# A fused block on one core: in self-attention's last round, the order of weights, values and gate products is changed

## The chip, the cores and the metric

The kernel runs on one core of a Trainium2 chip. The metric is device time in microseconds (us); three runs of the kernel before gave a median of 600.7 us (600.48 to 602.36). The core's engines have a queue of instructions each: TensorE (PE, matrix products; PEld is its loading of weights), VectorE (DVE), ScalarE (ACT), GpSimd (POOL) and SyncE (SP, which starts most transfers). They wait for each other by semaphores.

## The reference, cut to what matters

`x` has 64 time steps of 32 sequences with 256 channels, so 2048 rows; `ctx_768` holds 257 context rows for each time step.

```python
x = x + cross_attention(layernorm(x), ctx_768, ...)      # 16 heads
x = x + self_attention(layernorm(x), W, proj, concat_w, concat_b)
x = x + moe_ffn(layernorm(x), Wg, W1, b1, Wo, bo)         # 8 experts, top 2

def self_attention(inputs, W, proj, concat_w, concat_b):  # inputs (64, 32, 256)
    hp = tanh(einsum('sbh,hk->sbk', inputs, W))
    scores = einsum('sbk,k->sb', hp, proj)
    logits = where(s < t, scores[s, b], most negative float)
    attn = softmax(logits, axis=1)                        # over s
    context = einsum('tsb,sbh->tbh', attn, inputs)
    out = tanh(einsum('tbc,hc->tbh', concatenate([inputs, context], -1), concat_w) + concat_b)
    return out.at[:2].set(inputs[:2])
# moe_ffn starts with gate_logits = einsum('btd,ed->bte', x, Wg), softmax, top_k(2)
```

## The kernel before, in words

The program has three long stages: cross-attention (to 336 us of the profiled span), self-attention together with the gate of the experts (337 to 428 us, with the loads of the expert weights beside it), and the experts with the final sums. The change is in the second one, in a stretch of 13 us of it.

Self-attention takes the 2048 rows in four chunks of 512 (four tiles of 128 rows). All work is written as a pipeline of rounds `k = 0..5`, the same loop on each engine. In round k, chunk `c = k - 1` goes through attention and chunk `k - 2` through its third layernorm and the gate. Each engine works strictly through the order in which its calls are written; nothing reorders them but the code itself. So in round 4 the attention of the last chunk (chunk 3) and the gate of chunk 2 stand side by side, and in round 5 only the gate of chunk 3 and what follows it are left.

The pieces that the change touches, by their names in the code:

- On TensorE: `direct` (the product of the inputs with the first half of concat_w, left open in two PSUM banks), `crossed` (turns the attention weights Ab, four transposes), `mixed` (adds weights times values into the open banks: four matmuls; two increments of `u_o`, one for each half), `lifted` (turns the normed rows yn of a chunk for the gate, eight transposes in two halves), `gated` (the gate product, one half of it for each half of lifted), `turned_back` (turns its result gc, one transpose). Behind them in round 5 stand `slots(1)` (eight small matmuls that find the rows' positions), `busy(2)` (two matmuls with no use for the result, they only keep TensorE at work), `raised` (turns the last chunk's rows), `busy(1)`, `weighed` (the gate product of the last chunk), and `rank`.
- On VectorE: `weighted` (reciprocal and the product that makes Ab; waits for the exponentials), `values` (adds the bias to `products`' result and so makes Yv, two instructions), `positions` and `marks` (index arithmetic for the expert slots of a chunk two rounds earlier), `third` (adds self-attention's result to xb, then mean and variance), `best` and `chosen` (the top 2 of the gate).
- On ScalarE: `weights` (copies the turned weights to AT), `outs` (the two tanh of the result, zs), `gate_in` (copies the two halves of lifted to gh), `gate_out` (copies the gate product to gc).

For one chunk the way is: exponentials (ACT), weighted (DVE), crossed (PE), weights (ACT), mixed (PE), outs (ACT), third (DVE), scales (POOL). For the gate of a chunk: lifted, gate_in, gated, gate_out, turned_back, best.

PSUM has eight banks. Seven of them are given out in turn by a list, `plan`: the n-th tile of the list has bank n mod 7 and, before it is written, `take` waits for the semaphore with which the tile seven places before it was read out. The list and the order of the calls on TensorE have to agree.

At the end of the stage VectorE writes the list `inv` of rows by expert; GpSimd's first gather waits for it, and the experts for that gather.

Of the kernel before, what the change touches and what calls it, by code (L numbers as in the profile page):

```python
# [76 lines left out]
def build(nc, d, out, vx_d, w1_d, y_d, g_d):  # L77
    ctx = ExitStack()
    with ctx:
# [242 lines left out]
        u_ate = sem("u_ate")  # L322
# [45 lines left out]
        for k in range(6):  # L368
            c = k - 1
            if 0 <= c < 4:  # L370
                plan += [(("h", c, m), u_he, 2 * c + m + 1) for m in range(2)]
            if k < 4:
                plan += [(("t", k, h), u_tl, 2 * k + h + 1) for h in range(2)]
            if 0 <= c < 4:
                plan += [(("s", c), u_l, c + 1)]
            if k < 2:
                plan += [(("y", a, h), u_x, 2 * a + h + 1) for a, h in ahead[k + 1]]
            if 0 <= c < 4:
                plan += [(("Y", c, h), u_yb, 2 * c + h + 1) for h in range(2)]
            if 0 <= k - 3 < 2:  # L380
                plan += [(("r", k - 3), u_rk, k - 2)]
            if 0 <= c < 4:
                plan += [(("ay", c, h), u_z, 2 * c + h + 1) for h in range(2)]
            if k == 5:
                plan += [(("idle",), u_o, 8)]
            if 0 <= k - 2 < 4:
                plan += [(("t3", k - 2, h), f_hi, 2 * (k - 2) + h + 1) for h in range(2)]
            if 0 <= c < 4:
                plan += [(("at", c), u_ate, c + 1)]
            if 0 <= k - 2 < 4:  # L390
                plan += [(("g", k - 2), f_gl, k - 1)]
            if k == 5:
                plan += [(("r", 2), u_rk, 3), (("inv",), r_iv, 1)]
# [172 lines left out]
        with nc.Block() as block:  # L566
# [647 lines left out]
            def _(t):  # L1214
# [87 lines left out]
                def mixed(c):  # L1302
                    t.wait_ge(u_ate, c + 1)
                    t.wait_ge(u_yb, 2 * c + 2)
                    for h in range(2):
                        b = bank("ay", c, h)
                        for jj in range(2):
                            j = 2 * h + jj
                            mm = t.matmul(b[:, C * jj:C * jj + C], AT[:, j, :], Yv[:, j, :],
                                          start=False, stop=(jj == 1), skip_group_check=True)  # L1310
                        mm.then_inc(u_o, 1)
# [59 lines left out]
                for k in range(6):  # L1371
                    c = k - 1
                    if 0 <= c < 4:
                        hidden(c)
                    if 0 <= k - 4:
                        slots(t, k - 4)
                    if k < 4:
                        turned(k)
                    if 0 <= c < 4:
                        logits(c)  # L1380
                    if k < 2:
                        attended(ahead[k + 1])
                    if 0 <= c < 4:
                        products(c)
                    if 0 <= k - 3 < 2:
                        rank(t, k - 3, take("r", k - 3))
                    if 0 <= c < 4:
                        direct(c)
                    if k == 5:
                        take("idle")  # L1390
                        busy(2)
                        raised()
                        busy(1)
                        weighed()
                    if 0 <= k - 2 < 3:
                        lifted(k - 2)
                    if 0 <= c < 4:
                        crossed(c)
                    if 0 <= k - 2 < 3:
                        gated(k - 2)  # L1400
                    if 0 <= c < 4:
                        mixed(c)
                    if 0 <= k - 2 < 3:
                        turned_back(k - 2)
                b = take("r", 2)
# [14 lines left out]
            def _(v):  # L1420
# [38 lines left out]
                def final_norm(c):  # L1459

                    if c:
                        v.wait_ge(f_t, 2 * c)
                        v.wait_ge(f_yd, 16 * c + 16)
                    v.wait_ge(f_r, 3 * c + 2)
                    for j in range(2):
                        n = 4 * c + j
                        v.tensor_scalar(yn[:, j, :], xb[:, n, :], mv[:, n, 0:1], rs[:, n:n + 1],
                                        ALU.subtract, ALU.mult).then_inc(f_yv, 1)
# [8 lines left out]
                def values(c):  # L1477
                    for h in range(2):
                        v.wait_ge(u_yp, 2 * c + h + 1)
                        if c:  # L1480
                            v.wait_ge(u_o, 2 * c)
                        v.tensor_tensor(Yv[:, 2 * h:2 * h + 2, :], bank("Y", c, h)[:, :].rearrange("p (a c) -> p a c", a=2),
                                        bcc[:, 1, :].unsqueeze(1).broadcast_to([128, 2, C]), ALU.add).then_inc(u_yb, 1)
# [11 lines left out]
                def weighted(c):  # L1495
                    v.wait_ge(u_ex, 4 * c + 4)
                    link(v.reciprocal(sm[:, 2, :], sm[:, 1, :]))
                    v.wait_ge(u_az, 1)
                    if c:
                        v.wait_ge(u_at, c)  # L1500
                    for h in range(2):
                        r = slice(64 * h, 64 * h + 64)
                        v.tensor_tensor(Ab[r, :, 64 * h:64 * h + 64], L[r, :, :],
                                        sm[r, 2, :].unsqueeze(2).broadcast_to([64, 4, 64]), ALU.mult).then_inc(u_a, 1)
# [68 lines left out]
                for k in range(6):  # L1573
                    if 0 <= k - 2 < 4:
                        third(k - 2)
                    if k < 4:
                        lowered(k)
                    if 0 <= k - 1 < 4:
                        masked(k - 1)
                    if k < 4:  # L1580
                        kept(k)
                    if k == 5:
                        best(2)
                        chosen(2)
                        best(3)
                        chosen(3)
                    if 0 <= k - 2 < 2:
                        final_norm(k - 2)
                    if 0 <= k - 1 < 4:
                        weighted(k - 1)  # L1590
                        values(k - 1)
                    if 0 <= k - 3 < 2:
                        positions(v, link, k - 3, bank("r", k - 3))
                    if k == 5:
                        positions_of_two(v, link, bank("r", 2))
                    if k == 0:
                        added(((2, 0), (2, 1), (3, 0)))
                        moments(2)
                    if k == 1:
                        added(((3, 1),))  # L1600
                        moments(3)
                    if 0 <= k - 3:
                        marks(v, k - 3)
                    if 0 <= k - 2 < 2:
                        best(k - 2)
                        chosen(k - 2)
# [37 lines left out]
            def _(a):  # L1644
                a.wait_ge(s_ote, T)

                def normed(c):
                    a.wait_ge(u_rs, c + 1)
                    if c:
                        a.wait_ge(u_t, 2 * c)  # L1650
                        a.wait_ge(u_b2, c)
                    for j in range(2 * (c == 0), 4):
                        n = 4 * c + j
                        a.activation(xn[:, j, :], xb[:, n, :], ACT.Identity, bias=nb[:, 0, n:n + 1],
                                     scale=rs[:, n:n + 1]).then_inc(u_xn, 1)
# [61 lines left out]
                for k in range(6):  # L1717
                    if 0 <= k - 1 < 4:
                        squashed(k - 1)
                    if k < 4:  # L1720
                        highs(k)
                    if 0 <= k - 1 < 4:
                        exps(k - 1)
                    if 0 <= k - 2 < 3:
                        final_norm(k - 2)
                    if k + 1 < 4:
                        normed(k + 1)
                    if 0 <= k - 2 < 4:
                        gate_in(k - 2)
                    if k == 5:  # L1730
                        final_norm(3)
                    if 0 <= k - 1 < 4:
                        weights(k - 1)
                    if 0 <= k - 2 < 3:
                        gate_out(k - 2)
                    if 0 <= k - 1 < 4:
                        outs(k - 1)
                a.wait_ge(u_rf, 3)
                a.wait_ge(u_iv, 2)
# [326 lines left out]
```

## Time and profile before

| | |
|---|---|
| three runs, median (lowest to highest) | 600.7 us (600.48 to 602.36) |
| profiled execution: its time | 600.85 us |
| profiled execution: its span | 599.0 us |
| PE busy, share of the span | 583.1 us, 97% |
| DVE | 461.3 us, 77% |
| ACT | 351.0 us, 59% |
| POOL | 329.7 us, 55% |
| granted TensorE clock, mean | 0.994 |
| granted clock, 410 to 420 us and 420 to 430 us | 0.90 and 0.76 |

The 1.85 us between time and span lie around the recorded instructions. Matmul records overlap, so TensorE's share says that something was nearly always in it, not that it was at its peak; the filler matmuls of `busy` count as work too. An idle time in brackets at the end of a row is that of the engine just ahead of the instruction, with what ended it.

### The profile page before, as it was taken

How to read it: one execution, taken by the hardware profiler on the slowest of the kernel's cores; microseconds unless marked ns; L12 is line 12 of the kernel's file. 1: busy time of each engine (PE TensorE's matmuls, PEld its weight loads, DVE VectorE, ACT ScalarE, POOL GpSimd, SP SyncE). 2: the span in 40 equal slices, each digit the busy share in tenths (PEclk: the TensorE clock that was granted, in tenths of full speed). 3: DMA queues.
4: the chain of work that ended last, by engine and by line, in shares of the span. 5: the costliest groups of instructions: out<-in, count | busy, mean ns of one | idle time of the engine just before them, and what ended most of it. 6: DMA issues, size and time to landing. Idle time of an engine off the chain costs nothing.

```text
span 599.0 us, 21927 instructions
## 1 busy us (share of the span) xinstructions
PE 583.1 (97%) x8431; PEld 480.6 (80%) x8431; DVE 461.3 (77%) x1072; ACT 351.0 (59%) x768; POOL 329.7 (55%) x481
## 2 busy tenths in 40 slices
PE   8999999999999999999999999998899999999996
PEld 3888878888788888788888788886388878777695
DVE  4688867888678887677777687689778888887584
ACT  3677868878588888577777164545333333332462
POOL 3456867788668787678875222111346666664000
PEclk9999999999999999999999999999899999999999
DMA  8724553766544946693610399165424333344892
GB/s 230 182 68 119 149 188 94 242 162 213 153 148 147 264 118 219 167 247 125 210 41 4 125 435 400 65 204 198 156 95 132 133 131 134 130 131 126 314 343 75
DMA packets 65398, 102.13 MB, mean 170 GB/s; under 512 B 15280, under 2 KB 41968, under 8 KB 64400
## 3 DMA queue, kind: packets, MB, share of 16 engines
q1 hardware_dynamic: 59440, 84.59, 44.6%
q0 software_dynamic: 4992, 15.34, 7.7%
q8 instruction: 70, 1.15, 0.8%
q10 hardware_dynamic: 864, 0.79, 0.5%
q14 instruction: 32, 0.26, 0.1%
HBM read 69.43 MB, written 31.27 MB: 168 GB/s over the span
## 4 chain that ended last, share of the span: by engine, by line
PE 49%; POOL 20%; issue 15%; DVE 7%; DMA 4%; ACT 4%; DVEq 1%; POOLq 0%; SPq 0%; ACTq 0%
PE bank L1974 5%; PE bank L1048 5%; PE bank L1055 5%; PE bank L1080 4%; POOL hA L722 4%; POOL lA L718 4%; PE bank L2002 4%; POOL hA L714 4%; PE scores L1096 3%; PE scores L1069 3%; PE scores L1974 2%; DVE sg L1802 2%; DVE gg L1811 2%; PE scores L1232 2%; ACT sg L1916 2%
## 5 line engine op out<-in xcount | busy, mean ns | idle before, releaser
L854 DVE TENSOR_SCALAR Pm<-scores 128x514 f32<-128x514 f32 x128 | 88.1, 688 | 52.8 <-PE scores L1069 52.4
L970 ACT ACTIVATE Pm<-Pm,nm 128x257 f32<-128x257 f32 x256 | 115.8, 505 | 2.5 <-DVE nm L859 2.5
L859 DVE TENSOR_REDUCE nm<-Pm 128x2 f32<-128x514 f32 x128 | 87.5, 684 | 2.2
L965 ACT ACTIVATE PT<-bank 128x512 f32<-128x512 f32 x64 | 38.3, 598 | 74.3 <-PE bank L1080 74.3
L1048 PE MATMUL bank<-hA,wH 128*128 128x258 f32 x256 | 75.1, 304 | 0.3 <-POOL hA L722 0.3
L1080 PE MATMUL bank<-cst,Pm 128*128 128x128 f32 x512 | 70.0, 279 | 0.0
L1048 PE MATMUL bank<-hA,wL 128*128 128x258 f32 x256 | 69.2, 281 | 0.0
L1055 PE MATMUL bank<-wH,hA 128*128 128x256 f32 x256 | 68.9, 281 | 0.0
L1055 PE MATMUL bank<-wL,hA 128*128 128x256 f32 x256 | 68.8, 280 | 0.0
L1974 PE MATMUL bank<-W,xh 128*128 x208 | 66.8, 402 | 0.5 <-ACT xh L1904 0.5
L755 POOL TENSOR_TENSOR Mb<-Os,rc 128x64 f32<-128x64 f32 x64 | 21.8, 340 | 73.8 <-DVE rc L879 73.4
L1096 PEld LDWEIGHTS scores<-Vs,PT 128*32 128x32 f32 x4096 | 41.3, 110 | 26.1 <-issue 25.1
L1916 ACT ACTIVATE sg<-sg 128x512 f32<-128x512 f32 x39 | 24.7, 632 | 62.7 <-DVE sg L1802 62.7
L1789 POOL DMA_INDIRECT g_d<-gg,ds x39 | 38.6, 989 | 37.1 <-DVE gg L1811 37.1
L1080 PEld LDWEIGHTS bank<-cst,Pm 128*128 128x128 f32 x512 | 54.8, 140 | 2.8 <-issue 0.8
L948 ACT ACTIVATE kT<-bank,bcol 128x258 f32<-128x258 f32 x128 | 53.7, 470 | 2.9 <-PE bank L1048 2.6
L1778 POOL DMA_INDIRECT Xg<-y_d,inv x39 | 38.1, 977 | 24.3 <-DVE inv L1619 12.7
L1048 PEld LDWEIGHTS bank<-hA,wH 128*128 128x128 f32 x256 | 48.4, 189 | 1.5 <-issue 1.4
L1048 PEld LDWEIGHTS bank<-hA,wL 128*128 128x128 f32 x256 | 48.5, 190 | 0.2 <-issue 0.2
L1096 PE MATMUL scores<-Vs,PT 128*32 128x17 f32 x4096 | 47.8, 186 | 0.8 <-issue 0.6
L1055 PEld LDWEIGHTS bank<-wH,hA 128*128 128x128 f32 x256 | 48.1, 188 | 0.0
L1055 PEld LDWEIGHTS bank<-wL,hA 128*128 128x128 f32 x256 | 48.1, 188 | 0.0
(289 smaller groups left out, 1453.6 us busy)
## 6 DMA issues: line engine op xcount, KB each, us to landing
w_d<-whl SPq DMA_DIRECT2D x64, 256.0 KB, 3.6
W<-w_d SPq DMA_DIRECT2D x6, 2048.0 KB, 17.5
wst<-in_W1T SPq DMA_DIRECT2D x32, 256.0 KB, 3.8
cg<-g_d SPq DMA_DIRECT2D x16, 512.0 KB, 6.2
cx<-in_ctxT SPq DMA_DIRECT2D x31, 258.0 KB, 3.0
cx<-in_ctxT SPq DMA_DIRECT2D x62, 129.0 KB, 3.5
bb<-in_b SPq DMA_DIRECT2D x8, 512.0 KB, 6.5
W<-w_d SPq DMA_DIRECT2D x5, 512.0 KB, 5.2
```

The costliest lines, as they stand in the source:

```text
L854: v.tensor_scalar(Pm[:, i % 2, 2 * p:2 * p + 2, :], S4[:, 2 * p:2 * p + 2, 0:NK], -CLAMP, CLAMP, ALU.max, ALU.min).then_inc(s_cl, 1)
L859: v.tensor_reduce(nm[:, i % 2, 2 * p:2 * p + 2], Pm[:, i % 2, 2 * p:2 * p + 2, :], AX.X, ALU.max, negate=True).then_inc(s_nm, 1)
L948: a.activation(kT[:, i % 2, m, :], held("k", i, m)[:, 0:NKP], ACT.Identity, bias=bcol[:, 2 + m:3 + m]).then_inc(s_ke, 1)
L965: a.activation(PT[:, i % 2, 0, :, :].rearrange("p a b -> p (a b)"), held("p", i, 0)[:, :], ACT.Copy).then_inc(s_pte[0], 1)
L970: a.activation(Pm[:, i % 2, g, :], Pm[:, i % 2, g, :], ACT.Exp, bias=nm[:, i % 2, g:g + 1]).then_inc(s_ex, 1)
L1048: mm = t.matmul(b[:, 0:NKP], w[:, 128 * m:128 * m + 128], c, start=(e == 0), stop=(e == 4))
L1055: mm = t.matmul(b[:, C * c:C * c + C], x[:, 128 * c:128 * c + 128], w[:, C:2 * C], start=(e == 0), stop=(e == 4))
L1080: mm = t.transpose(b[:, o:o + 128], Pm[:, i % 2, 2 * p + gg, 128 * c:128 * c + 128], ident)
L1096: mm = t.matmul(pO[r, VH * g:VH * g + VH], PT[:, i % 2, p, 2 * gg + c, r], Vs[:, i % 4, c, 4 * (h // 2) + g, h % 2, :], start=first, stop= ...
L1778: g.indirect_dma_start(out=Xg[:, i % 4, :], out_offset=None, in_=y_d, in_offset=bass.IndirectOffsetOnAxis(ap=inv[:, i:i + 1], axis=0)).the ...
L1789: g.indirect_dma_start(out=g_d, out_offset=bass.IndirectOffsetOnAxis(ap=ds[:, i:i + 1], axis=0), in_=gg[i % 3][:, :], in_offset=None).then ...
L1974: mm = t.matmul(o, x[:, i % 3, k, :], W1[:, bass.DynSlice(w + (part * 2048 + k * 1024 + 512 * h), 512)], start=(k == 0 and part == 0 and x ...
```

## The change

Three things are written in another order, and nothing is computed otherwise. On TensorE, in round 4, `crossed(3)` and `mixed(3)` stand ahead of `lifted(2)` and `gated(2)`; before, the order was lifted(2), crossed(3), gated(2), mixed(3). `turned_back(2)` stays behind all of them. The plan of the banks is changed to agree. On VectorE `values(3)` stands ahead of `weighted(3)`. On ScalarE `weights(3)` and `outs(3)` stand ahead of `gate_in(2)`; `gate_out(2)` now follows gate_in(2) directly.

```diff
--- before.py
+++ after.py
@@ -383,9 +383,11 @@
                 plan += [(("ay", c, h), u_z, 2 * c + h + 1) for h in range(2)]
             if k == 5:
                 plan += [(("idle",), u_o, 8)]
+            if k == 4:
+                plan += [(("at", c), u_ate, c + 1)]
             if 0 <= k - 2 < 4:
                 plan += [(("t3", k - 2, h), f_hi, 2 * (k - 2) + h + 1) for h in range(2)]
-            if 0 <= c < 4:
+            if 0 <= c < 3:
                 plan += [(("at", c), u_ate, c + 1)]
             if 0 <= k - 2 < 4:
                 plan += [(("g", k - 2), f_gl, k - 1)]
@@ -1392,14 +1394,17 @@
                         raised()
                         busy(1)
                         weighed()
-                    if 0 <= k - 2 < 3:
+                    if 0 <= k - 2 < 2:
                         lifted(k - 2)
                     if 0 <= c < 4:
                         crossed(c)
-                    if 0 <= k - 2 < 3:
+                    if 0 <= k - 2 < 2:
                         gated(k - 2)
                     if 0 <= c < 4:
                         mixed(c)
+                    if k == 4:
+                        lifted(2)
+                        gated(2)
                     if 0 <= k - 2 < 3:
                         turned_back(k - 2)
                 b = take("r", 2)
@@ -1586,8 +1591,11 @@
                         chosen(3)
                     if 0 <= k - 2 < 2:
                         final_norm(k - 2)
+                    if k == 4:
+                        values(3)
                     if 0 <= k - 1 < 4:
                         weighted(k - 1)
+                    if 0 <= k - 1 < 3:
                         values(k - 1)
                     if 0 <= k - 3 < 2:
                         positions(v, link, k - 3, bank("r", k - 3))
@@ -1725,15 +1733,18 @@
                         final_norm(k - 2)
                     if k + 1 < 4:
                         normed(k + 1)
+                    if k == 4:
+                        weights(3)
+                        outs(3)
                     if 0 <= k - 2 < 4:
                         gate_in(k - 2)
                     if k == 5:
                         final_norm(3)
-                    if 0 <= k - 1 < 4:
+                    if 0 <= k - 1 < 3:
                         weights(k - 1)
                     if 0 <= k - 2 < 3:
                         gate_out(k - 2)
-                    if 0 <= k - 1 < 4:
+                    if 0 <= k - 1 < 3:
                         outs(k - 1)
                 a.wait_ge(u_rf, 3)
                 a.wait_ge(u_iv, 2)
```

TensorE, the end of round 4 and the start of round 5, the kernel before (yn: lifted; Ab: crossed; gh with a 32-row result: gated; Yv,AT: mixed; gc: turned_back; A_114,Bv: slots(1); cst alone: busy; xb: raised):

```order
L1343 MATMUL bank<-cst,yn 128x128 x4
L1343 MATMUL scores<-cst,yn 128x128 x4
L1299 MATMUL scores<-cst,Ab 128x128 x4
L1351 MATMUL scores<-gh,WgT 32x128 x8
L1309 MATMUL bank<-Yv,AT 128x256 x4
L1362 MATMUL scores<-cst,gc 128x128
L436 MATMUL bank<-A_114,Bv 128x128 x8
L1367 MATMUL scores<-cst 128x512 x2
L1320 MATMUL bank<-cst,xb 128x128 x8
```

The same place in the changed kernel:

```order
L1301 MATMUL bank<-cst,Ab 128x128 x4
L1311 MATMUL bank<-Yv,AT 128x256 x4
L1345 MATMUL scores<-cst,yn 128x128 x8
L1353 MATMUL scores<-gh,WgT 32x128 x8
L1364 MATMUL scores<-cst,gc 128x128
L438 MATMUL bank<-A_114,Bv 128x128 x8
L1369 MATMUL scores<-cst 128x512 x2
L1322 MATMUL bank<-cst,xb 128x128 x8
```

The turned weights and their product have moved to the front; the three steps of the gate (yn, gh, gc) now follow each other with nothing between them, and slots, fillers and raised stand behind them as before.

ScalarE at the same place, before (yn: final_norm(2); gh: gate_in; AT: weights; gc: gate_out; zs: outs):

```order
L1664 ACTIVATE yn<-xb,nb,rs 128x256 x4
L1714 ACTIVATE gh<-bank 128x512
L1714 ACTIVATE gh<-scores 128x512
L1693 ACTIVATE AT<-scores 128x512
L1700 ACTIVATE gc<-scores 128x128
L1707 ACTIVATE zs<-bank 128x512 x2
L1714 ACTIVATE gh<-bank 128x512 x2
```

and in the changed kernel:

```order
L1672 ACTIVATE yn<-xb,nb,rs 128x256 x4
L1701 ACTIVATE AT<-bank 128x512
L1715 ACTIVATE zs<-bank 128x512 x2
L1722 ACTIVATE gh<-scores 128x512 x2
L1708 ACTIVATE gc<-scores 128x128
L1722 ACTIVATE gh<-bank 128x512 x2
```

The copy of the weights and both tanh have moved ahead of the two copies for the gate of chunk 2.

## Rows read from the trace of the kernel before

**Rows 1.** The page, busy time of TensorE: us, share, instructions

```profile
PE 583.1 (97%) x8431; PEld 480.6 (80%) x8431; DVE 461.3 (77%) x1072; ACT 351.0 (59%) x768; POOL 329.7 (55%) x481
```

**Rows 2.** Waits of 400 to 436 us: us in total, times, longest

```profile
POOL Xg L1778 <- DVE inv L1619: 12.7, 1, 12.7
```

**Rows 3.** Chain that ended last, 400 to 434 us: start us, us, what

```profile
400.29 3.07 PE scores L1278 x24
...
408.58 1.99 PE bank L1309 x8
...
411.33 1.77 PE scores L1367 x4
413.10 0.87 PE bank L1320 x8
413.97 0.86 PE scores L1367 x2
414.83 1.70 PE bank L1331 x16
...
418.93 3.60 PE scores L1367 x4
```

**Rows 4.** Timeline of VectorE, 402 to 418 us: start us, us, instruction, idle before

```profile
404.40 0.18 DVE L1497 RECIPROCAL sm<-sm 128x4 f32<-128x4 f32 x1 [1.50 <-ACT L L1686]
...
405.51 1.29 DVE L1482 TENSOR_TENSOR Yv<-scores,bcc 128x512 f32<-128x512 f32 x2
...
410.19 0.68 DVE L497 TENSOR_TENSOR A<-i,rf 128x512 f16<-128x512 f16 x1
410.79 1.41 DVE L1511 SCALAR_TENSOR_TENSOR xb<-zs,cst,xb 128x512 f32<-128x512 f32 x2
...
413.71 0.16 DVE L1534 COPY gl<-scores 128x32 f32<-128x32 f32 x1
...
416.62 0.19 DVE L1527 TENSOR_TENSOR gl<-bank,um 128x32 f32<-128x32 f32 x1 [0.34 <-PE bank L1331]
```

**Rows 5.** Timeline of ScalarE, 404 to 414 us

```profile
404.27 2.06 ACT L1664 ACTIVATE yn<-xb,nb,rs 128x256 f32<-128x256 f32 x4
406.95 0.60 ACT L1714 ACTIVATE gh<-bank 128x512 f32<-128x512 f32 x1 [0.62 <-PE bank L1343]
407.45 0.59 ACT L1714 ACTIVATE gh<-scores 128x512 f32<-128x512 f32 x1
407.92 0.60 ACT L1693 ACTIVATE AT<-scores 128x512 f32<-128x512 f32 x1
408.58 0.28 ACT L1700 ACTIVATE gc<-scores 128x128 f32<-128x128 f32 x1
409.75 0.60 ACT L1707 ACTIVATE zs<-bank 128x512 f32<-128x512 f32 x1 [0.89 <-PE bank L1309]
410.61 0.60 ACT L1707 ACTIVATE zs<-bank 128x512 f32<-128x512 f32 x1 [0.27 <-PE bank L1309]
```

**Rows 6.** Timeline of TensorE, matmuls and weight loads, 406 to 419 us

```profile
406.32 0.60 PE L1343 MATMUL bank<-cst,yn 128*128 128x128 f32 x4
...
407.19 0.60 PE L1299 MATMUL scores<-cst,Ab 128*128 128x128 f32 x4
...
408.09 0.16 PEld L1351 LDWEIGHTS scores<-gh,WgT 128*32 128x32 f32 x8 [0.21 <-ACT gh L1714]
...
410.20 0.14 PEld L1362 LDWEIGHTS scores<-cst,gc 128*128 128x128 f32 x1
...
410.41 0.27 PE L1362 MATMUL scores<-cst,gc 128*128 128x128 f32 x1
...
410.93 0.23 PEld L436 LDWEIGHTS bank<-A,Bv 128*128 128x128 f16 x4 [0.19 <-DVE A L497]
...
418.58 0.21 PE L420 MATMUL scores<-csum,O 128*128 128x40 f16 x1 [1.91 <-DVE Mk L1550]
```

**Rows 7.** Stretches: us, busy PE, PEld, DVE, ACT, POOL, granted clock, DMA, GB/s

```profile
418.00:424.40 6.40, 5.72 (x20) 2.62 (x20) 5.03 (x16) 2.72 (x8) 0.00 (x0) 0.50 0.72 267
424.40:424.80 0.40, 0.40 (x2) 0.00 (x0) 0.40 (x1) 0.40 (x2) 0.00 (x0) 0.52 0.89 359
...
432.00:434.00 2.00, 0.88 (x4) 0.63 (x5) 0.99 (x4) 0.72 (x2) 1.39 (x3) 1.00 0.25 78
```

## The prediction

> **What bounds the kernel now.** First the page: TensorE is busy for 97% of the span [rows 1], and so it stays open whether it is late in the stretch of the change, since its filler matmuls count as work. The waits of 400 to 436 us answer what a microsecond there is worth: GpSimd's first gather sits for 12.7 us until VectorE has `inv` [rows 2], and the experts start behind it. So what moves the end of the gate moves the end of the kernel by the same amount, and the question is only which engine brings that end.
>
> The chain of waits then shows the stretch itself. From 408.58 it is TensorE without a break up to weighed: mixed(3), slots(1), busy(2) 1.77 us, raised 0.87, busy(1) 0.86, weighed 1.70, which ends at 416.53 [rows 3]. VectorE comes to best(3) and waits 0.34 us for it [rows 4]. VectorE's own timeline is nearly full: there is one hole, 1.50 us ahead of the reciprocal at 404.40, until the exponentials are there [rows 4]. So there are two lines side by side, TensorE's is the later one, by 0.34 us, and that is the lever: TensorE's line can be lengthened at full price and VectorE's shortened for nothing.
>
> **Values ahead of weights on VectorE.** values(3) needs products(3), which in the chain run from 400.29 to 403.36 [rows 3]. Its two instructions take 1.29 us together [rows 4]. The hole begins at 404.40 - 1.50 = 402.90. Half 0 starts there; half 1 would start at about 403.54, after 403.36, and ends at 402.90 + 1.29 = 404.19, ahead of 404.40. So the hole takes it up whole, Ab comes no later, and everything on VectorE behind it is free 1.29 us sooner. marks(1) ends at 410.19 + 0.68 = 410.87 in the trace [rows 4]; it would end at 409.58. TensorE's wait of 0.19 us for it in slots(1) [rows 6] goes. If the cover fails (half 1 late by as much as its whole 0.65), Ab is late by 0.44, still ahead of TensorE: weighted has the time from its reciprocal at 404.40 to values at 405.51 [rows 4], so Ab would be there at 405.95, and TensorE asks for it at 406.3. So price 0, gain 0.19 on TensorE's line.
>
> **Weights turned and mixed first.** The four transposes of Ab take the place of lifted's first four, at 406.32, and are done 0.60 later at 406.92 [rows 6]. ScalarE is free then (yn ends at 404.27 + 2.06 = 406.33), and takes what comes from there at 406.95 as gh did [rows 5]. AT ends 0.60 later, at 407.55; in the trace it ends at 408.52 and mixed begins at 408.58 [rows 3, 5]. So mixed begins at 407.61, 0.97 sooner, and ends at 409.60 instead of 410.57. The two tanh follow at 409.75 - 0.97 = 408.78 and 410.61 - 0.97 = 409.64. So outs(3) is 0.97 sooner, and third(3) can begin when marks ends. What is paid is an idle TensorE from 406.75 (four transposes are issued in half of 407.19 - 406.32 = 0.87 for eight [rows 6]) to 407.61, which lifted and gated filled before.
>
> **The gate of chunk 2 last.** This is the part that costs. Its three steps go to ScalarE and back twice, and before, the turned weights and mixed lay between them on TensorE. Now:
> - lifted(2): eight transposes behind mixed, 409.60 + 0.87 = 410.47 for the second half.
> - gate_in(2): ScalarE has the second tanh until 410.24. Instructions in a row start 0.50 and 0.47 apart there (406.95, 407.45, 407.92 [rows 5]), so half 0 starts at 410.12, half 1 at 410.60 and ends at 411.20.
> - gated(2): its second half began 408.09, 0.05 behind its copy, and gc began at 408.58 [rows 5, 6]: 0.49. So it begins at 411.25, and gc runs from 411.74 to 412.02.
> - turned_back(2): weight load at 410.20 to end of matmul at 410.41 + 0.27 = 410.68 is 0.48 in the trace [rows 6], but part of that was the queue of mixed; 0.27 alone is the least, 0.48 the most. I take 0.38, half way: with 0.05 for the signal it ends at 412.45, where it ended at 410.68. TensorE is 1.77 us later.
> - Behind it slots(1) no longer waits: -0.19. From there on raised finds its input: third's sums begin at 409.6 and take 1.41 [rows 4], so they are there at 411.0, and raised comes at 413.10 + 1.58. Fillers, raised and weighed move as one block, ScalarE's last gate_in is asked for nothing in between, and weighed ends at 416.53 + 1.58 = 418.11.
>
> VectorE gets to best(2) at 413.71 - 1.29 = 412.42 [rows 4], needs turned_back's result at 412.45 and so is just in time; then it waits about 3 us for weighed instead of 0.34. The 1.29 us won there are spent in this wait.
>
> **The other effects** have no price: the expert weights that wait for mixed(3) start 0.97 sooner; the last final_norm comes behind gate_in(3), about 0.6 later, and its store is hidden by all that lies between weighed and the gather (rank, marks, slots, inv); banks taken in the new order were read out long ago, except those of values, which come sooner.
>
> **Sum.** 1.77 - 0.19 = 1.58, so +1.6 us. The profiled execution took 600.85, 0.15 above the median; against the median of 600.7 the forecast is 602.3. The terms that I could not read (turned_back 0.27 to 0.48, five hand-overs of 0.05 that may be 0.03 to 0.1, the start of a mixed that comes out of an idle TensorE, -0.1 to +0.2) give +1.3 to +2.0 with the clock where it is.
>
> A rule speaks here. TensorE sat idle 1.91 us ahead of rank(3) at 418.58, although the fillers behind it wait for nothing [rows 3, 6]: matmuls keep their order. The Trainium skill, TensorE: Matmul & The Clock Gate, section "Step-by-step: what each phase is for", says the same: only weight loads are pulled ahead, matmuls stay in program order. If ready work could pass, slots(1) and the fillers would lie in the gate's waits, and the change would win; by the rule, and the trace agrees, they can't.
>
> **The clock.** It is the part that the sum can't hold. The granted clock is 0.50 from 418.0 to 424.4 and comes back at about 424.8; before it fell TensorE had done weighed's short matmuls and then stood idle [rows 6, 7]. It stayed at 1.00 over 432 to 434 with TensorE busy for only 0.88 of 2.00 us [rows 7]. Busy(2) behind rank(3) takes 3.60 us at half clock and 1.77 at full [rows 3].
>
> **Rivals.**
> (a) VectorE sets the end. Then its 1.29 us come through, and time falls to 600.7 - 1.3 = 599.4: not slower. For it: VectorE has no other hole, and is only 0.34 behind. Against it: it decides only if TensorE's line is no longer than before less 0.95, that is if gate_in, gated and gate_out don't stand between mixed and slots(1); in the new order they do.
> (b) The clock falls in the new gaps. From 406.75 to 412.1 TensorE now has idle pieces of about 0.86, 0.4, 0.1 and 0.4 us, with short matmuls between. If it is at half speed by 412, busy(2) costs +1.8, raised and busy(1) about as much again (0.87 + 0.86, twice as long), so +3.6 above the sum, less up to 0.5 if it is then at full speed behind rank(3): 605.4 to 605.9; half of it if only busy(2) is hit: 604.1. Against it: more idle time than in any one of these pieces was survived at 432 to 434. The same page, section "What's actually happening", says that the throttled state is the default and that activity releases it; the direction is that of the rows, and by it (b) is what more idle time risks.
> (c) The shift is partly given back behind rank(3). There, at half clock, busy(2) ends at 418.93 + 3.60 = 422.53; with the clock falling later in relation to the work, up to 0.5 us of it and of the slots behind it returns: +1.1, 601.8, no change that can be told.
>
> **How the numbers follow.** I give the sum (+1.1 to +2.2 with (c)'s give-back mixed in, 601.8 to 602.9) 0.60, (c) alone or the sum's steps overlapping better than I think 0.12, (a) 0.13, (b) 0.15. About 0.3% (1.8 us) is what a measurement of this kernel tells from no change; the line is at 602.5, just above the forecast. Of the first case 0.24 lies above it and 0.36 below; with (b) slower has 0.39. Faster needs less than 598.9, which (a) reaches only with 0.5 more from the clock: 0.07. Same has 0.54. The range reaches from (a)'s side at 600.3 to (b)'s small form at 604.1; the likeliest case's own is 601.6 to 603.1.
>
> **What would show it.** Right: zs at about 408.8 and 409.6; the reciprocal on VectorE without idle time of more than 0.2 ahead of it; L1364's matmul at about 412.2, raised's first at about 414.5; VectorE waiting about 3 us ahead of the last gl. Wrong: VectorE waiting for nothing there; a granted clock below 1.00 between 408 and 417; TensorE's turned_back earlier than 411.5.

## The result and the profile after

| | before | changed |
|---|---|---|
| 20 runs each, median | 601.21 us | 603.23 us |
| lowest to highest | 599.69 to 603.43 | 600.77 to 605.79 |
| profiled execution, span | 599.0 us | 603.2 us |

The ratio is 1.003, 95% interval 1.0017 to 1.0043; on 601.2 us that is +1.8 us, between +1.0 and +2.6. The forecast was +1.6. The change makes the kernel slower by about 0.3%.

The changed kernel came to products(3) 0.48 us later in this profile, 400.77 by the chain instead of 400.29 [rows 3], in a part of the program that is the same in both. Times below are read less this 0.48 where they are set against the old ones.

The chain of waits of the changed kernel, from crossed(3) to VectorE's last gl (start us, us, what):

```profile
400.77 3.07 PE scores L1280 x24
...
406.96 0.45 PE bank L1301 x4
...
407.44 0.61 ACT AT L1701
...
408.09 2.01 PE bank L1311 x8
...
410.61 0.60 ACT gh L1722
411.21 0.14 issue
411.35 0.87 PE scores L1353 x16
...
412.24 0.29 ACT gc L1708
...
412.57 0.33 PE scores L1364
412.90 0.45 PE bank L438 x8
413.34 1.77 PE scores L1369 x4
415.12 0.87 PE bank L1322 x8
415.99 0.86 PE scores L1369 x2
416.85 1.70 PE bank L1333 x16
...
418.64 0.20 DVE gl L1532
```

Where the old chain was TensorE alone from mixed(3) on [rows 3], this one leaves it twice behind mixed(3), for gh and for gc. Less the offset, mixed(3) begins 0.97 sooner (408.09 - 0.48 = 407.61), and turned_back(2) ends at 412.90 - 0.48 = 412.42 instead of 410.68 [rows 6]. The last gl stands at 418.64 - 0.48 = 418.16 instead of 416.62 [rows 4]: +1.54.

VectorE's timeline, changed kernel (start us, us, instruction, idle before):

```profile
403.30 1.28 DVE L1487 TENSOR_TENSOR Yv<-scores,bcc 128x512 f32<-128x512 f32 x2
404.88 0.18 DVE L1502 RECIPROCAL sm<-sm 128x4 f32<-128x4 f32 x1 [0.31 <-ACT L L1694]
...
409.47 0.68 DVE L499 TENSOR_TENSOR A<-i,rf 128x512 f16<-128x512 f16 x1
410.08 1.43 DVE L1516 SCALAR_TENSOR_TENSOR xb<-zs,cst,xb 128x512 f32<-128x512 f32 x2
...
413.01 0.16 DVE L1539 COPY gl<-scores 128x32 f32<-128x32 f32 x1
...
418.64 0.19 DVE L1532 TENSOR_TENSOR gl<-bank,um 128x32 f32<-128x32 f32 x1 [3.05 <-PE bank L1333]
```

The hole of 1.50 us has become 0.31, third begins 1.19 sooner (410.08 - 0.48 = 409.60 instead of 410.79), and all of it is lost again in the last row: the wait of 0.34 has grown to 3.05.

TensorE's rows at its three waits, changed kernel:

```profile
408.09 2.00 PE L1311 MATMUL bank<-Yv,AT 128*128 128x256 f32 x8 [0.69 <-ACT AT L1701]
...
411.35 0.82 PE L1353 MATMUL scores<-gh,WgT 128*32 128x128 f32 x16 [0.39 <-ACT gh L1722]
...
412.57 0.33 PE L1364 MATMUL scores<-cst,gc 128*128 128x128 f32 x1 [0.40 <-ACT gc L1708]
```

At the same places the kernel before waited 0.33 for AT and 0.21 for gh, in its weight loads, and not at all for gc.

The granted clock of the changed kernel (us, busy PE, PEld, DVE, ACT, POOL, clock, DMA, GB/s):

```profile
410.00:412.00 2.00, 1.61 (x25) 1.06 (x23) 2.00 (x5) 1.57 (x3) 0.00 (x0) 1.00 0.50 94
412.00:414.00 2.00, 1.60 (x19) 1.04 (x12) 1.97 (x20) 0.28 (x1) 0.75 (x2) 1.00 0.90 365
...
418.00:425.00 7.00, 3.22 (x28) 1.81 (x28) 5.58 (x28) 2.62 (x7) 0.00 (x0) 1.00 0.79 240
425.60:429.00 3.40, 3.08 (x12) 1.41 (x11) 2.78 (x8) 1.95 (x6) 0.00 (x0) 0.51 0.14 57
```

It was 1.00 in every 2 us from 408 to 418, the new waits included. It did not fall behind weighed, as it had [rows 7], but some 7 us later, and then lay on slots(3) and the last fillers.

### The profile page after: what moved, and what is told of

The parts are those of the page before. It is cut to its first block, busy times and chain, and to the rows that moved or that the text cites. A ratio compares the mean times of both kernels' runs of the same rounds, so it can differ in the third digit from the quotient of the medians.

```text
span 603.2 us, 21927 instructions
## 1 busy us (share of the span) xinstructions
PE 583.0 (97%) x8431; PEld 480.5 (80%) x8431; DVE 461.0 (76%) x1072; ACT 350.8 (58%) x768; POOL 329.3 (55%) x481
## 4 chain that ended last, share of the span: by engine, by line
PE 51%; POOL 20%; issue 14%; DVE 5%; DMA 4%; ACT 3%; DVEq 0%; POOLq 0%; SPq 0%; ACTq 0%
PE bank L1985 7%; PE bank L1050 5%; PE bank L1057 5%; PE bank L1082 4%; POOL hA L724 4%; POOL lA L720 4%; PE bank L2013 4%; POOL hA L716 4%; PE scores L1985 3%; PE scores L1098 3%; PE scores L1071 3%; DMA Xg<-y_d,inv 2%; PE scores L1234 2%; POOL Mb L757 2%; POOL tm L748 2%
```

## Experiments

One measure serves all of them: from the first products(3) matmul of TensorE's timeline to the start of VectorE's last gl, the instruction that takes over the gate product of the last chunk; and the same to `inv`. The expectations count from the chain's piece, which begins 0.07 later for the kernel before, so that their 16.33 is 16.40 here.

| kernel | products to gl | VectorE's wait ahead of gl | products to inv |
|---|---|---|---|
| before, two profiles | 16.40, 16.44 | 0.34, 0.34 | 27.65, 27.69 |
| changed, two profiles | 17.94, 17.94 | 3.05, 3.04 | 29.54, 28.78 |
| e1 values alone | 16.22 | 0.35 | 27.46 |
| e2 without values | 17.94 | 1.86 | 29.19 |
| e3 slots in the gap | 17.44 | 2.56 | 29.01 |
| e4 changed, no filler | 16.17 | 1.28 | 27.42 |
| e5 before, no filler | 16.13 | none | 27.38 |
| e7 lifted between | 15.92 | 1.01 | 27.18 |
| e8 the same, one filler | 15.06 | none | 25.92 |
| e9 the same, no filler | 14.94 | none | 25.81 |
| r4, e7 again | 15.93 | 1.02 | 27.45 |
| r3, e9 again | 14.93 | none | 25.80 |

The first four (e1 to e4) ran beside 35 runs of the kernel before that spread from 605.0 to 615.8 us, so their ratios (0.9981, 0.9982, 0.998 and 0.9961, each with an interval of about 0.3% to either side) tell nothing about effects of this size: e2's stands against what its trace says, and e4's, the only one whose interval stays clear of 1, says 2.4 us less where its trace says 0.2. For them only the measure of the trace is used.

**e1: values alone.**

```diff
 # the kernel before, VectorE
+                    if k == 4:
+                        values(3)
                     if 0 <= k - 1 < 4:
                         weighted(k - 1)
+                    if 0 <= k - 1 < 3:
                         values(k - 1)
```

> The kernel before with one part of the change: values(3) ahead of weighted(3) on VectorE; TensorE and ScalarE as before. Measure: from the first products(3) matmul to VectorE's last gl copy (before 416.62 - 400.29 = 16.33 us, changed kernel 418.64 - 400.77 = 17.87). Theory 1 (TensorE's line sets the end): 16.33 - 0.19 (slots(1) no longer waits for marks(1)) = 16.1, and VectorE waits longer than 0.34 ahead of gl. Theory 2 (VectorE sets the end): its 1.3 us come through, 15.0. Time: theory 1 about -0.2, same; theory 2 -1.3 us.

Measured: 16.22, by 0.18 to 0.22 less than before: theory 1. But the second half of the expectation failed: VectorE's wait did not grow, it is 0.35. Its timeline tells why:

```profile
411.08 1.54 DVE L1511 SCALAR_TENSOR_TENSOR xb<-zs,cst,xb 128x512 f32<-128x512 f32 x2 [0.76 <-ACT zs L1710]
...
417.07 0.19 DVE L1527 TENSOR_TENSOR gl<-bank,um 128x32 f32<-128x32 f32 x1 [0.35 <-PE bank L1331]
```

With values moved and mixed(3) where it was, third stands waiting for the tanh. The two halves of the change belong together on VectorE: the one frees it, the other brings its input.

**e2: all but values.**

```diff
 # the changed kernel, VectorE
-                    if k == 4:
-                        values(3)
                     if 0 <= k - 1 < 4:
                         weighted(k - 1)
-                    if 0 <= k - 1 < 3:
                         values(k - 1)
```

> The changed kernel with values(3) put back behind weighted(3); only the orders on TensorE and ScalarE are changed. Theory 1: the same measure stays at 17.9, since TensorE comes to slots(1) at about 412.9, two microseconds behind marks(1); VectorE's wait ahead of gl falls from 3.05 to about 1.8. Theory 2: 17.9 + 1.3 = 19.2. Time: theory 1 as the changed kernel, some 1.6 to 2 us above before; theory 2 some 3.

Measured: 17.94 with a wait of 1.86, as theory 1 had it. The order of values changes nothing at gl; the loss is all in TensorE's and ScalarE's order. Nor do slots(1) wait for marks(1) here, though values(3) stand behind weighted(3): TensorE comes to them at 412.01, when VectorE has been in third since 410.57.

**e3: ready work put into one of the waits.**

```diff
 # the changed kernel, TensorE; slots(0) stays where it was
                     if k == 4:
                         lifted(2)
+                        slots(t, 1)
                         gated(2)
```

> The changed kernel with one more edit: slots(1), eight matmuls that take 0.45 us, stands between lifted(2) and gated(2) instead of behind turned_back(2). Theory 1 (what is lost is TensorE's idle time while the gate of chunk 2 goes to ScalarE and back): 17.87 - 0.45 = 17.4, and the wait of 0.39 us ahead of gated is gone. A rival, that the loss comes from ScalarE being late for the gate (its copies behind the two tanh) and not from TensorE's queue, has the same gl time as the changed kernel, 17.9, since gated's copies come no sooner. Time: -0.45 against the changed kernel.

Measured: 17.44, 0.50 less. The rival, ScalarE late for the gate, had 17.9: gated begins 10.64 us after products(3) here and 10.65 in the changed kernel, so its copies come no sooner, and the time is won all the same. In the timeline gated has no wait left in the matmuls, while turned_back keeps its own:

```profile
409.26 0.61 PE L438 MATMUL bank<-A,Bv 128*128 128x128 f16 x8
409.81 0.82 PE L1353 MATMUL scores<-gh,WgT 128*32 128x128 f32 x16
411.04 0.33 PE L1364 MATMUL scores<-cst,gc 128*128 128x128 f32 x1 [0.40 <-ACT gc L1709]
```

**e4 and e5: the fillers as a probe.** The same edit on both kernels; it lengthens or shortens only TensorE's line.

```diff
                         take("idle")
-                        busy(2)
                         raised()
```

> The changed kernel without the two filler matmuls (1.77 us) between slots(1) and raised. Theory 1: TensorE's line sets the end, all of the fillers lies on it, 17.87 - 1.77 = 16.1; VectorE's wait ahead of gl falls from 3.05 to 1.3. Theory 2 (VectorE sets the end): no change, 17.9. If TensorE's clock falls because of the missing fillers, weighed and what follows take up to twice as long, and the measure is 17 or more.

> The kernel before without the two filler matmuls (1.77 us) between slots(1) and raised. From the first products(3) matmul to the last gl copy it took 16.33 us. Theory 1: VectorE is only 0.34 us behind TensorE there, so no more than 0.34 is gained, 16.0, and VectorE doesn't wait ahead of gl; the same edit on the changed kernel gains all of the 1.77. Rival (fillers are free wherever they stand, the clock is what they are for): 16.3 or more, with the granted clock at 0.50 earlier than 417.

Measured: 16.17 for the changed kernel, 1.77 less, as much as the fillers take, with VectorE's wait down from 3.05 to 1.28; 16.13 for the one before, 0.27 to 0.31 less, with VectorE not waiting. What a shorter TensorE line can win is the time for which VectorE waits for it: about 3 us in the changed kernel, a third of a microsecond before. In e4 the clock was at 1.00 up to 416.6, behind the last gl at 415.89. e5's time is 0.9992 (0.9976 to 1.0007), no change that can be told.

**e7: the same goal with the waits filled.**

```diff
 # the changed kernel, TensorE (round 4)
                     if 0 <= c < 4:
                         crossed(c)
+                    if k == 4:
+                        lifted(2)
                     ...
                     if 0 <= c < 4:
                         mixed(c)
                     if k == 4:
-                        lifted(2)
                         gated(2)
+                        slots(t, 1)
 # slots(1) is taken out of its old place, as in e3
 # ScalarE
                     if k == 4:
                         weights(3)
-                        outs(3)
                     if 0 <= k - 2 < 4:
                         gate_in(k - 2)
+                    if k == 4:
+                        outs(3)
```

> The changed kernel with the waits filled: TensorE does crossed(3), lifted(2), mixed(3), gated(2), slots(1), turned_back(2); ScalarE does weights(3), gate_in(2), outs(3), gate_out(2). lifted(2), 0.87 us, lies in the time in which AT is copied, mixed(3) in the time of gate_in(2), slots(1) in that of gate_out(2). Theory 1: mixed(3) begins as early as in the changed kernel, and TensorE has no wait left, so it gains the waits of the kernel before as well (0.17 and 0.21 ahead of gated, 0.33 ahead of mixed, 0.19 in slots): the measure is about 15.9 to 16.1, against 16.33 before and 17.87 changed. If the loss were in mixed(3) ahead of the gate as such, or in the clock, it stays near 17.9.

Measured: 15.92. Its timeline of TensorE has no wait from crossed to raised:

```profile
405.35 0.60 PE L1301 MATMUL bank<-cst,Ab 128*128 128x128 f32 x4
405.79 1.04 PE L1345 MATMUL scores<-cst,yn 128*128 128x128 f32 x8
406.66 1.97 PE L1311 MATMUL bank<-Yv,AT 128*128 128x256 f32 x8
408.56 0.65 PE L1353 MATMUL scores<-gh,WgT 128*32 128x128 f32 x16
409.14 0.62 PE L438 MATMUL bank<-A,Bv 128*128 128x128 f16 x8
409.60 0.33 PE L1364 MATMUL scores<-cst,gc 128*128 128x128 f32 x1
409.77 1.88 PE L1369 MATMUL scores<-cst 128*128 128x512 f32 x4
```

mixed(3) is as early as in the changed kernel (7.41 us after products(3), there 7.39), and the gate isn't late: the loss was not in mixing first, but in standing idle for it. What each of the three moves (lifted, slots(1), gate_in) is worth by itself was not tried. Time: 0.9995 (0.9979 to 1.001).

**e8 and e9: fewer fillers with it.**

```diff
 # e7's kernel; e8 keeps busy(1), e9 none
                         take("idle")
-                        busy(2)
+                        busy(1)
                         raised()
```

> As the kernel with lifted(2) between crossed(3) and mixed(3), with one filler matmul instead of two ahead of raised. Theory 1: 0.88 less on TensorE's line, 15.1, about where VectorE gets to by itself (its values are 1.3 us sooner and third is no longer held by outs): the first edit in which the VectorE gain comes through; time about 1.2 us below the kernel before, if the clock stays.

> As above with no filler ahead of raised. Theory 1: VectorE sets the end now, at about 15.1, so the second filler gives nothing more than 0.1 to 0.3; with the clock falling earlier, it costs. If VectorE isn't the limit, 14.3.

Measured: 15.06 and 14.94, both with VectorE not waiting ahead of gl. The first filler gave 0.86, the second 0.12: here the end of the gate goes over from TensorE to VectorE, and e9's VectorE runs without a wait from third to gl:

```profile
408.34 1.41 DVE L1517 SCALAR_TENSOR_TENSOR xb<-zs,cst,xb 128x512 f32<-128x512 f32 x2
411.26 0.16 DVE L1540 COPY gl<-scores 128x32 f32<-128x32 f32 x1
413.87 0.19 DVE L1533 TENSOR_TENSOR gl<-bank,um 128x32 f32<-128x32 f32 x1
```

In e5, where VectorE sets the end too, third began 10.60 us after products(3); here it is 9.41, and the 1.19 between them is the 1.19 by which e9 is shorter than e5.

Times: e8 0.9959 (0.9946 to 0.9972, nine runs), e9 0.9953 (0.9936 to 0.9971, six runs); e9's median is 597.96 us against 601.2 before. Both beat the kernel before, e8 by 2.5 us where 1.2 was expected. Not all of it is the gate: of the 1.84 us by which e9 has inv sooner, 1.46 lie ahead of gl, and 0.38 behind it (10.87 us from gl to inv instead of 11.25), where the low stretch of the clock fell otherwise.

**The repeats.**

> The kernel before, unchanged, profiled again: what differs between two profiles of one kernel. The way from the first products(3) matmul to inv should again be 27.6 to 27.7 us, and from the first gather to the end 170.6 us plus or minus what the chip varies.

> The changed kernel, unchanged, profiled again beside the one before. Theory 1: the whole effect lies between products(3) and inv (29.5 us against 27.65), and the 1.83 us that its first profile was longer behind the first gather (172.47 against 170.64) are not of the change; then this profile has 170.5 to 171 there. Rival: the change also slows the experts, and 172.5 comes again. Time +1.7 to +1.9 us against before.

> The filled order without filler ahead of raised once more, for its time: products to gl 14.9, products to inv 25.8, 1.8 less than before; time 0.3 to 0.5% below before, with the clock at 1.00 until past 417.

> The filled order with both fillers once more: products to inv 27.2, that is 0.45 less than before; time about 0.1% below before, not to be told from it.

Measured: before again 0.9996 (0.998 to 1.0013), changed again 1.003 (1.0016 to 1.0045), the version without filler 0.9963 (0.9951 to 0.9976), both fillers 0.999 (0.9974 to 1.0006). The result and the improvement stand in a second set of runs. Products to inv is 27.69, 28.78, 25.80 and 27.45. Ahead of gl all came as expected; three expectations failed behind it. Inv came at 28.78 instead of 29.5 in the changed kernel and at 27.45 instead of 27.2 with both fillers, and without filler the clock fell between 416 and 417 (0.57 there) and not past 417. From the first gather to the end it is 171.21 for before (170.64 the first time) and 171.56 for the changed kernel (172.47): so most of the 1.83 us by which the first two profiles differed there did not come again, though neither 170.5 to 171 nor 172.5 was met. That the change costs nothing at all behind the gather is not shown; the timed +1.8 and the mean shift of inv, (29.54 + 28.78 - 27.65 - 27.69) / 2 = +1.49, agree within the interval.

The repeat of the changed kernel has the clock at another place:

```profile
418.00:421.00 3.00, 1.76 (x21) 1.65 (x20) 1.22 (x14) 1.69 (x4) 0.00 (x0) 1.00 0.18 58
422.00:425.00 3.00, 3.00 (x4) 0.98 (x4) 2.73 (x9) 1.46 (x5) 0.00 (x0) 0.50 0.62 237
425.40:431.00 5.60, 4.47 (x26) 2.43 (x26) 4.42 (x14) 2.42 (x7) 0.00 (x0) 1.00 0.33 136
```

Here it was low while VectorE and ScalarE made the inputs of slots(2), and full again for slots(3) and the last fillers: gl to inv took 28.78 - 17.94 = 10.84 us, against 11.60 in the first profile and 11.25 before. The same program, 0.76 us apart. What the low stretch costs depends on what it lies on. In the kernel before it lay on the fillers behind rank(3) and on slots(2):

```profile
421.76 0.72 ACT L507 ACTIVATE A<-A,cst 128x512 f16<-128x512 f16 x1
422.63 1.01 PE L436 MATMUL bank<-A,Bv 128*128 128x128 f16 x8
```

and in the changed kernel's first profile on neither:

```profile
423.74 0.72 ACT L509 ACTIVATE A<-A,cst 128x512 f16<-128x512 f16 x1
424.60 0.64 PE L438 MATMUL bank<-A,Bv 128*128 128x128 f16 x8 [1.88 <-ACT A L509]
```

The fillers at half clock cost next to nothing, although the chain runs through them [rows 3]: slots(2) begin 6.01 us after gl before and 5.98 in the repeat, with the fillers at half clock, and 5.96 in the first profile, with them at full clock, since they wait for ScalarE's copies in any case. Slots(2) at half clock do cost: the next copies on ScalarE begin 7.06 us after gl before, 6.63 and 6.65 in the changed kernel. From there to inv it is 4.19, 4.97 and 4.19: the low stretch on slots(3) and the last fillers cost 0.78.

## Why the prediction was right, point by point

- **TensorE's line sets the end, by 0.34 us.** Right, and shown by one edit on two kernels: without fillers the changed kernel gained 1.77, the one before about 0.3 (e4, e5). Rival (a), VectorE sets the end, is out for the changed kernel, and comes true only when TensorE's line is made shorter (e5, e8, e9).
- **values(3) fit into the hole.** Right: the reciprocal was not late. They start where the hole starts; 0.31 us of it is left, more than the 0.2 that was given as the most.
- **mixed(3) 0.97 sooner, tanh at 408.78 and 409.64.** Measured less the offset: 407.61, 408.77 and 409.64.
- **The gate's way to ScalarE and back costs 1.77.** Measured 412.42 - 410.68 = 1.74. The term that I had to place between bounds, turned_back alone, took 0.33, from 412.57 - 0.48 = 412.09 to 412.42, and 0.38 counted with the hand-over; assumed were 0.38 alone and 0.43 with it. Of these 0.05, 0.02 were lost ahead of it, so 1.77 was 0.03 too high. e2 shows that this order alone is the loss, e3 and e7 that it is TensorE's idle time in it.
- **-0.19 in slots(1).** Measured -0.21: turned_back's end to the first filler is 0.44 against 0.65. The size is right, the reason only for the kernel before, where e1 shows it (0.18 to 0.22). In the changed one the wait is gone whatever the order of values, as e2 shows: TensorE comes 1.7 us later. So the moved values had no part in what the change did at gl.
- **Sum +1.58 at gl.** Measured +1.54.
- **The clock.** It did not fall in the new gaps, so rival (b) did not come. What the sum could not hold, its place behind rank(3), added 0.35 between gl and inv in one profile and gave back 0.41 in the other. Rival (c) was half right: a give-back of 0.4 was there in both, but out of slots(2) alone and not out of busy(2), whose half speed hid behind ScalarE; and in one of the two the low stretch took 0.78 again further on, which nothing in the forecast had. The time, +1.8, lies 0.2 above the forecast, which is no difference that the interval (+1.0 to +2.6) can tell.
- **The range.** Its lower end, 600.3, was said to reach from (a)'s side, but (a)'s own time was 599.4 and lay outside. It did not matter here.
- **In-order matmuls.** e3 and e7 bear the rule out from the other side: ready work filled the waits as soon as it was written ahead of them, and not before.

## What to carry to other kernels

An earlier start for one chain is paid with whatever stood between its steps: before moving a step forward, look which hand-overs to other engines it was covering, and put ready work of the same engine there (e7: the same early mix, no wait). Filler matmuls on a line with little slack are a probe for the slack of the others; and parts that win nothing to be told by the time alone (values, the filler) won 0.4% together with the filled order, so measure such parts together as well as apart. That values are needed for it is argued from VectorE's timelines (e5 against e9); e9 without them was not run.

## What the runs showed of the hardware that was not expected

The stretch at half clock moves from run to run of the same program: 421.9 to 425.2 us in one profile of the changed kernel, 425.6 to 429.0 in the other, although both have the same idle time of 1.9 us ahead of rank(3); in the kernel before it was low from 418 to 424.4. It is worth up to 0.76 us here, over 40% of the effect that was to be measured. What makes it fall where it does is open.

In e1 to e4 the experts took 174.7 to 178.9 us from the first gather to the end, where all other profiles have 170.1 to 172.5. A good part of the time shows as TensorE waiting for the gathers. The waits of 436 to 560 us of e1 (us in total, times, longest), which in the kernel before came to 2.4 and 0.5 us:

```profile
PEld scores L1959 <- DMA Xg<-y_d,inv: 10.8, 11, 2.3
PE scores L1959 <- DMA Xg<-y_d,inv: 6.2, 7, 1.9
```

The two rows came to 10.5 to 17.1 us together in e1 to e4 and to at most 4.9 in the other profiles. These four ran on another chip than the later sets; whether that is the reason is open. Kernels of that set could be told apart in the stretch of the change only, not by their times.
